# Asking for the experts' down weights from ScalarE instead of SyncE

## The reference, cut to what matters

```python
# x: (4, 512, 256) f32; E = 64 experts, M = 176, H = 256, capacity C = 96
h = layernorm(x) * (1 + ca) + sa
x = x + ga * attention(h)                 # 16 heads of 128
h = layernorm(x) * (1 + cb) + sb
# router: softmax over 64 experts, 3 of 8 groups, top 6 experts of a token
slot = flat * C + minimum(pos, C - 1)     # pos: place of the token in its expert's queue
buf  = zeros(E * C, H).at[slot].set(h[tok]).reshape(E, C, H)
g = einsum('ech,emh->ecm', buf, Wg)
u = einsum('ech,emh->ecm', buf, Wu)
out = einsum('ecm,ehm->ech', silu(g) * u, Wd).reshape(E * C, H)
y = sum_k out[slot] * topk_w[..., None]
shared = silu(h @ Sg.T) * (h @ Su.T) @ Sd.T
return x + gb * (y + shared)
```

## Time and profile before

| what | value |
|---|---|
| median of 3 runs | 1059.94 us (1058.62 to 1061.05) |
| profiled execution, its own time | 1062.05 us |
| its span, first to last instruction | 1060.3 us |
| PE busy | 986.5 us (93%) |
| DVE busy | 681.8 us (64%) |
| ACT busy | 581.2 us (55%) |
| POOL busy | 405.3 us (38%) |
| DMA engines' mean busy share, 887 to 993 us | 1.09 |
| moved, 887 to 993 us | 280 GB/s |

### The profile page before, as it was taken

How to read it: one execution, slowest core, us unless ns; L and a number is a source line. 1 busy time by engine, 2 the same in 40 slices (tenths; PEclk the granted TensorE clock), 3 DMA queues, 4 the chain that set the end, 5 groups by cost and what they waited for, 6 DMA issues and landing times.

```text
span 1060.3 us, 18375 instructions
## 1 busy us (share of the span) xinstructions
PE 986.5 (93%) x6301; PEld 875.3 (83%) x6301; DVE 681.8 (64%) x1815; ACT 581.2 (55%) x1093; POOL 405.3 (38%) x599
## 2 busy tenths in 40 slices
PE   4999999999999999999999999999979799999973
PEld 4799999999999999999999999999854465555542
DVE  3566667778778877877887787787468132222356
ACT  2566766766676676667667666766531033333320
POOL 2222223233224654322465432246515434545550
PEclk9899999999999999999999999999999899999985
DMA  9992000001000110100010012000023179999947
GB/s 352 330 322 75 0 0 1 1 1 56 1 1 22 38 38 32 56 1 1 22 37 32 19 56 87 2 9 22 3 88 110 34 205 291 285 278 281 245 73 237
DMA packets 65288, 99.30 MB, mean 94 GB/s; under 512 B 8271, under 2 KB 46426, under 8 KB 64824
## 3 DMA queue, kind: packets, MB, share of 16 engines
q1 hardware_dynamic: 47128, 79.61, 24.5%
q0 software_dynamic: 11808, 12.87, 6.0%
q10 hardware_dynamic: 6272, 5.79, 1.9%
HBM read 66.11 MB, written 38.86 MB: 99 GB/s over the span
## 4 chain that ended last, share of the span: by engine, by line
PE 67%; DVE 11%; DMA 9%; issue 6%; ACT 3%; POOL 2%; another core or an unknown queue 1%; SPq 0%; POOLq 0%; DVEq 0%; ACTq 0%
PE ps L1290 22%; PE ps L1343 11%; PE ps L1316 11%; DMA acc<-wos,arena 8%; PE ps L1331 7%; PE ps L1496 3%; PE ps L1299 2%; PE ps L1302 2%; PE ps L1323 2%; PE ps L1511 2%; PE ps L1449 1%; ACT prob L605 1%; DVE arena L957 1%; DVE bst L764 1%
## 5 line engine op out<-in xcount | busy, mean ns | idle before, releaser
L448 POOL TENSOR_TENSOR holdp<-neghalf 128x1 f32<-128x1 f32 x145 | 31.5, 217 | 465.3 <-ACT prob L611 241.1
L605 ACT ACTIVATE prob<-ps,rn 128x512 f32<-128x512 f32 (+3 forms) x256 | 121.0, 526 | 124.3 <-PE ps L1316 116.5
L1290 PE MATMUL ps<-wh,hth 128*128 128x384 f32 x512 | 178.3, 348 | 5.5 <-DVE htl L790 3.4
L1290 PE MATMUL ps<-wh,htl 128*128 128x384 f32 x512 | 173.0, 338 | 0.0
L1290 PE MATMUL ps<-wl,hth 128*128 128x384 f32 x512 | 172.8, 338 | 0.0
L838 DVE TENSOR_REDUCE ss<-arena 128x8 f32<-128x1024 f32 x64 | 78.1, 1220 | 128.5 <-ACT arena L581 128.2
L1343 PE MATMUL ps<-vx,prob 128*128 128x129 f32 (+1 forms) x1280 | 153.5, 274 | 0.4 <-POOL prob L496 0.4
L1343 PEld LDWEIGHTS ps<-vx,prob 128*128 128x128 f32 x1280 | 148.6, 191 | 0.7 <-POOL prob L496 0.7
L581 ACT ACTIVATE arena<-ps 128x1024 f32<-128x1024 f32 x64 | 65.7, 1026 | 123.8 <-PE ps L1290 123.8
L560 POOL DMA_INDIRECT acc<-wos,arena x64 | 91.9, 1436 | 104.2 <-ACT wos L725 86.9
L502 POOL DMA_INDIRECT slot_rows<-pay,arena x96 | 97.7, 1017 | 44.5 <-issue 24.6
(11 more groups left out here) (194 smaller groups left out, 2234.6 us busy)
## 6 DMA issues: line engine op xcount, KB each, us to landing
wge<-in_wgu SPq DMA_DIRECT2D x30, 352.0 KB
slot_rows<-pay SPq DMA_DIRECT2D x1, 6456.0 KB, 36.0
acc<-pay SPq DMA_DIRECT2D x3, 2048.0 KB, 19.5
arena<-slot_rows ACTq DMA_DIRECT2D x56, 100.9 KB
warena<-in_wqkv SPq DMA_DIRECT2D x1, 4992.0 KB, 20.8
wde<-in_wd SPq DMA_DIRECT2D x24, 192.0 KB
prob<-in_wgu SPq DMA_DIRECT2D x12, 352.0 KB
arena<-in_wgu SPq DMA_DIRECT2D x12, 352.0 KB
```

The source lines that it names most:

```text
L605: act_(prob[:, OFF[j]:OFF[j] + w], sflat[:, OFF[j]:OFF[j] + w], ACT.Tanh, scale=rn[:, bass.ds(head(n), 1), TT + j:TT + j + 1].squeeze(1)). ...
L1290: last = mm(ps[:, i, 0:3 * DH], hp[:, k, i * P:(i + 1) * P], wp[:, k, :], start=(k == 0 and m == 0), stop=(k == KC - 1 and m == 2))
```

## The change

SP's function `down(e)` and its call are taken out. ACT gets `e_down(e)` with the same wait and the same transfer, called at step `e` for expert `e - 2`, behind `e_orow(e-2)` and ahead of `e_rows(e+6)`. The transfers, 53 in number, so go through ACT's queue, in which before only the slot rows were, and each stands in it directly ahead of one load of slot rows. Sizes, places and semaphores stay.

```diff
@@ SP
-            def down(e):
-                sp.wait_ge(s["dn_ps"], e + 1)
-                sp.dma_start(wds[e % RING], wd[e + RING]).then_inc(w_in[e % RING], 16)
-
@@ SP, loop over e
                 if e >= 2:
-                    if e - 2 + RING < E:
-                        down(e - 2)
                     last_row(e - 2)
@@ ACT
+            def e_down(e):
+
+                a.wait_ge(s["dn_ps"], e + 1)
+                a.dma_start(wds[e % RING], wd[e + RING]).then_inc(w_in[e % RING], 16)
+
@@ ACT, e_period(e, base)
                     e_orow(e - 2, base) if e >= 2 or isinstance(base, int) else e_orow(e - 2 + XR, base - XR)
+                if e >= 2 and e - 2 + RING < E:
+                    e_down(e - 2)
                 if XR <= e + LEAD < E:
                     e_rows(e + LEAD)
```

## The result

The changed kernel takes 1054.64 us (median of 10 runs, 1050.87 to 1058.02), the kernel before beside it 1061.07 us (10 runs, 1057.61 to 1064.67). The ratio is 0.9943, with a 95% interval from 0.9924 to 0.9962, so 6.4 us of 1061.07. The forecast was 1061.4 us within 1055.0 to 1067.5 us. The profiled execution of the changed kernel took 1056.7 us, its span is 1055.0 us. One run further down, one of e3b's, took 1423.8 us at a granted clock of 0.653 where its others have 0.973 to 0.978, and is left out of the ratio there.

A forecast was written before the change was run, and what follows sets the result against it. The prediction took scatters, paced by full DMA engines, to bound the middle stretch. All terms were 0 except +1.5 us for the scatters' landing, giving 1061.4 us from a median of 1059.94 us, range 1055.0 to 1067.5 us.

The forecast's parts named there:

- What bounds the kernel: Middle stretch, 887 to 993 us: scatters set the pace, 2.78 us each, with the DMA engines full at 280 GB/s.
- SP's issues: SP loses 53 issues of 0.43 us, some 23 us, but lies on no path of the chain; nothing gained.
- ACT's issues: ACT gets 53 issues of 0.36 us, 19 us in all, covered by its idle time; cost taken as 0.
- the later request: Down weights asked for 2 us later but used eleven experts, 31 us, on; cost 0.
- the slot rows: Slot rows stand behind 192 KB of weights on ACT's queue, landing up to 1.8 us later; cost 0.
- The scatters' landing: Deciding term: each landing between 0.41 us less and 0.41 us more, taken as +0.10 us, +1.5 us over 45 intervals.
- Rival 1: Scatters wait for pieces of both SP's and ACT's queues, 0.137 us more per expert, 6.2 us: 1066.1 us; chance 0.25.
- Rival 2: SP's queue runs empty, scatters land sooner, 288 GB/s, 6.5 us gained: 1053.4 us, half of it 1056.7; chance 0.22.
- Rival 3: Slot rows land over 14.9 us after the request and scatters wait; 1065.5 us for one us beyond; chance 0.10.

The follow-up runs named there:

- e3b: Second run of the changed kernel with slot rows issued ahead of the down weights on ACT's queue; ratio 0.994 to the kernel before.
- e9: Kernel before with only half of each expert's down weights loaded from expert 11 on; ratio 0.9832, 1035.33 against 1050.86 us.
- e7: Kernel before with down weights asked for one expert later, still on SP directly behind the gate and up weights; ratio 1.000.
- e4: Kernel before with slot rows too on SP's queue, behind the last row, ACT's queue left empty; ratio 1.002.
- a2: The change run again unaltered, beside e12 on one chip; ratio 0.9918 to the kernel before, 1052.43 us.
- e8: Kernel before with down weights asked for as early, but issued ahead of the gate and up weights on SP; ratio 0.997.
- e14: Kernel before with down weights on SP waiting for one more gate and up multiplication, so issued between two gate/up loads; ratio 0.9971.
- e1: Kernel before with the down weights' request moved behind the last row on SP: ahead of gate/up, an expert later; ratio 0.9962.
- a3: The change run once more unaltered, beside e1b on one chip; ratio 0.9919 to the kernel before, 1044.13 us.
- e1b: The kernel of e1 run again, beside the change on one chip; ratio 0.997 to the kernel before, 1048.05 us.
- e13: Kernel before with weights split by expert between SP's and ACT's queues, down still directly behind gate/up; ratio 0.9987.
- e6: Mirror of the change: gate and up weights on ACT's queue ahead of the slot rows, down weights on SP; ratio 0.9982 to the kernel before.
- e10: Kernel before with ACT issuing the slot rows ahead of the output row, weights untouched; ratio 0.9974.
- e12: The change with both of ACT's transfers, down weights and slot rows, ahead of the output row; ratio 0.9958 to the kernel before, 1057.1 us.
- b2: The kernel before run again unaltered for a second trace; 1064.15 us, 2.85 us between scatters.

## Why the prediction was wrong, by its steps

- **What bounds the kernel**: right. Scatters pace the loop, full DMA engines pace the scatters. e9 shows it: fewer bytes, and the loop falls back to PE's 2.39 us.
- **SP's issues, ACT's issues, the later request, the slot rows: cost 0**: right, with less room than thought where ACT and the slot rows are concerned. Output rows keep 2.39 us at PE's pace. A later request alone is 1.000 (e7). ACT's copy moved by 0.71 us and not by 0.36. The slot rows show a single wait of 0.3 us.
- **The scatters' landing, +0.10 us, 45 intervals, +1.5 us**: this is the step that failed. Measured over two traces before and three with the change, the interval fell by 0.14 us, which is 0.42 us on a landing: the lower end of the term (0.41 us less), where I took a quarter of the upper one. (The first pair of traces alone has 0.07 us, no more than two traces of the kernel before differ by.) That end was set equal to the upper one without a row for it, so that it fits is luck. The reason for my choice was that an expert moves 759 kB and that 280 GB/s is what the engines can do, so that 2.71 against 2.78 us leaves no room. The 280 GB/s was read as a capacity and was an outcome. At a share of 1.08 to 1.10 in every kernel that moves all bytes, the rate in one stretch goes from 273 (e4) to 300 GB/s (a2), by when and behind what a transfer is issued. A busy share of 1 says that packets are always in work, not how long each takes. The page of the kernel before had a sign of it: 352, 330 and 322 GB/s in the first three slices of 26.5 us, where larger loads run, at 0.92 in the first of them.
- **Rival 1, turns**, at 1066.1 us: refuted in sign. The wait for turns that I worked out, longer with two full queues, isn't seen: the landing became shorter. The Trainium skill (DMA: Bandwidth & Descriptors, "Queues, rings and completion order") has each engine go round the queue rows that it has work for. That isn't contradicted here, and not borne out either, since no row shows turns.
- **Rival 2, faster**, 1053.4 us and half of it 1056.7 us: the measured 1054.64 us lies between. Its price was worked out from a rate that the trace had shown over a stretch (288 GB/s). That came near, but it is no bound: 90 us at 300 GB/s were seen in a2. Its reason, that SP's queue runs empty between two transfers, isn't shown; it isn't needed for a gain, for e8 and e14 gain with all weights still in that queue. So the price is met in part by luck. It had 0.22, and the lower end of the range, 1055.0 us, cut off its last part, though the mechanism was open in sign.
- **Rival 3, late slot rows**: did not occur beyond the single wait of 0.3 us.

What the runs show of the cause: the bytes set the pace (e9), and down weights sent directly behind gate and up weights in SP's queue, at the landing that releases the scatter, cost 0.3% (e8 against the kernel before; e1, e1b and e14 agree, and e7, which keeps that order, gains nothing). The change gains more than that (a3 beside e1b). Two queues by themselves gain little (e13, e6). What stays open is why full engines carry more in one order than in another, and whether the change's further gain is due to ACT's queue or to the moment at which ACT asks: no run has the down weights on SP's queue at the moment at which the change asks for them. The slot rows' place in the queue isn't isolated in e6 either.

## What to carry to other kernels

Where the DMA engines are full, GB/s at that share isn't a ceiling: before costing a moved transfer at nothing, leave the bounds open on both sides, on the faster one at least by the best rate in the trace, and give that side its weight. Where a load that isn't urgent stands directly behind a larger one, at the event that also releases the critical small transfer, try the other order, a gap, or the other queue, each of which is a few lines. Look up in the trace when the moved transfer really goes out: in e14 and e10 it wasn't when the edit meant it to. Compare on one chip, and use several traces before reading a difference of 2% in a rate.

## What wasn't expected of the hardware

- The rate of full engines depends on the order in which two loads of 352 and 192 KB are issued from one queue: 291 against 274 GB/s on one chip (e8, e7), with DMA share 1.10 in both. In the times that is 1049.17 against 1052.37 us.
- Asking earlier for some of the slot rows, 101 KB each, gained 0.26% with nothing else changed (e10), and a kernel that asks at another moment for both transfers of ACT's queue took 4.7 us more than the change beside it (e12, a2).
- The same kernel takes 1061 to 1062 us on three chips and 1051 to 1052 us on two. The loop over the experts begins earlier there: the first scatter is at 849.17 us in e7 and 857.12 us in b2. Up to about 818 us the two traces run alike. Then, in the shared expert, ACT (L695) stands idle for 6.88 us and DVE (L1115) for 10.64 us in b2, by a wait whose releaser the profile gives only as "remote", PE is busy for only 1.13 us of those from 835 to 840 us, and from 835 to 845 us the granted clock is 0.50 (1.2 GHz) there and 1.00 (2.4 GHz) in e7. All 14 traces with a first scatter behind 856 us have such waits, the six with one ahead of 851 us have none. What they are waits for is open. Among the 14 the first scatter comes between 856.94 and 859.79 us, so that up to 3 us of a difference between two single executions can lie ahead of the loop.
